# Head 0's row maxima moved forward into the projection stage of a fused attention and expert kernel

## The reference, cut to what matters

```python
mod = (silu(c) @ wmod).reshape(2, 6, 1, -1)
sa, ca, ga, sb, cb, gb = (mod[:, i] for i in range(6))
h = layernorm(x) * (1 + ca) + sa                 # x: (2, 2048, 256)
Q, K, V = lora_linear(h, ...)                    # W x + b + 2 * B(A x), 16 heads of 16
attn = softmax(Q @ K.T / 4); x = x + ga * lora_linear(attn @ V, ...)
h = layernorm(x) * (1 + cb) + sb
x = x + gb * (shared_ffn(h) + routed_ffn(h))     # each row to one of 8 experts
```

## Time and profile before

| | us |
|---|---|
| median of 3 runs (lowest, highest) | 1971.74 (1971.08, 1971.88) |
| the profiled execution, its own time | 1971.86 |
| its span, first to last instruction | 1969.9 |
| busy: TensorE, VectorE, ScalarE, GpSimd | 1867.0, 1570.3, 1244.8, 344.1 |
| one reduce of a 128x512 tile (mean of 2048) | 0.682 |

### The profile page before, as it was taken

The page is one execution under the profiler, slowest core; times in us unless marked ns, Lnnn a source line. Parts: engine busy times, 40 slices in busy tenths (PEclk is TensorE's granted clock), DMA queues, the critical chain, the costliest instruction groups (busy, mean ns, idle before and its releaser), DMA issues.

```text
span 1969.9 us, 34636 instructions
## 1 busy us (share of the span) xinstructions
PE 1867.0 (95%) x13114; PEld 769.8 (39%) x13115; DVE 1570.3 (80%) x2738; ACT 1244.8 (63%) x1423; POOL 344.1 (17%) x429
## 2 busy tenths in 40 slices
PE   8796999999999999999999999999984899999997
PEld 5441222222222222222222222222224655589996
DVE  6765999999999999999999999999826632245553
ACT  5353777777777777777777777777871221144442
POOL 6562200000000000000000000000015622223332
PEclk9997999999999999999999999999997899999998
DMA  5432111111111111111111111111047432322221
GB/s 183 142 129 59 42 41 42 61 55 42 41 54 59 46 41 43 59 57 42 42 54 58 50 39 39 57 54 42 7 150 226 160 102 96 113 82 73 72 72 48
DMA packets 88657, 141.53 MB, mean 72 GB/s; under 512 B 11928, under 2 KB 59032, under 8 KB 88520
## 3 DMA queue, kind: packets, MB, share of 16 engines
q1 hardware_dynamic: 72424, 101.61, 16.0%
q0 software_dynamic: 11072, 32.80, 5.0%
q10 hardware_dynamic: 5024, 5.24, 0.8%
HBM read 90.84 MB, written 48.51 MB: 71 GB/s over the span
## 4 chain that ended last, share of the span: by engine, by line
PE 83%; DVE 10%; DMA 2%; ACT 2%; issue 2%; POOL 1%; SPq 1%; POOLq 0%; DVEq 0%; ACTq 0%
PE ps L943 24%; PE ps L932 20%; PE ps L909 15%; PE ps L1621 7%; DVE mx L999 6%; PE ps L1172 5%; PE ps L1644 3%; PE ps L1506 3%; PE ps L619 2%; DMA l_in<-inverse_sums 2%; PE ps L628 1%; ACT prob L1024 1%; DVE x_t L451 1%; DVE x L1258 1%; PE ps L977 0%
## 5 line engine op out<-in xcount | busy, mean ns | idle before, releaser
L999 DVE TENSOR_REDUCE mx<-ps 128x1 f32<-128x512 f32 x2048 | 1273.7, 682 | 59.5 <-PE ps L909 56.2
L1024 ACT ACTIVATE prob<-ps 128x1024 f32<-128x1024 f32 x1024 | 992.4, 1021 | 275.1 <-PE ps L932 272.6
L943 PE MATMUL ps<-prob,vs 128*32 128x512 f32 x4096 | 546.4, 605 | 0.7 <-ACT prob L1024 0.7
L909 PE MATMUL ps<-k_high,q_high 64*128 64x512 bf16 x2048 | 399.8, 387 | 10.4 <-DVE mx L999 10.4
L932 PE MATMUL ps<-q_high,k_high 64*128 64x512 bf16 x2048 | 390.2, 378 | 15.4 <-issue 12.5
L932 PE MATMUL ps<-q_low,k_low 34*128 34x512 bf16 x2048 | 390.5, 378 | 0.0
L909 PEld LDWEIGHTS ps<-k_high,q_high 64*128 64x128 bf16 x2048 | 99.0, 92 | 646.8 <-DVE mx L999 623.0
L1078 POOL CAST mb<-turned_sb 16x128 bf16<-16x128 f32 x32 | 8.9, 279 | 934.2 <-ACT turned_sb L1037 892.9
L932 PEld LDWEIGHTS ps<-q_low,k_low 34*128 34x128 bf16 x2048 | 100.0, 94 | 117.0 <-issue 0.7
L932 PEld LDWEIGHTS ps<-q_high,k_high 64*128 64x128 bf16 x2048 | 101.5, 96 | 101.6 <-ACT prob L1024 30.0
L943 PEld LDWEIGHTS ps<-prob,vs 128*32 128x32 f32 x4096 | 80.7, 108 | 118.7 <-issue 113.4
(11 more groups left out here) (152 smaller groups left out, 1431.0 us busy)
## 6 DMA issues: line engine op xcount, KB each, us to landing
k_high<-qk_parts SPq DMA_DIRECT2D x126, 128.0 KB
qk_parts<-parts SPq DMA_DIRECT2D x32, 384.0 KB, 3.1
k_low<-qk_parts SPq DMA_DIRECT2D x128, 64.0 KB
head_out<-head_out_sb SPq DMA_DIRECT2D x32, 256.0 KB, 10.8
q_high<-qk_parts SPq DMA_DIRECT2D x126, 64.0 KB
sorted_in<-zero_row POOLq DMA_DIRECT2D x13, 390.0 KB, 7.3
xs<-sorted_in SPq DMA_DIRECT2D x39, 130.0 KB
q_low<-qk_parts SPq DMA_DIRECT2D x64, 64.0 KB
```

Source lines behind the costliest of these rows:

```text
L909: pe.matmul(ps[:, ring.bank((n, m, u)), :], q_high[p][mine, t * P:(t + 1) * P], k_high[p][mine, c * CH:(c + 1) * CH], start=True, stop=Tru ...
L943: mm = pe.matmul(ps[32 * j:32 * j + 32, 7, :], vs[buf(h)][:, kt, :], prob[:, kt % 2, j * CH:(j + 1) * CH], start=(kt == 0), stop=(kt == KT ...
L999: dve.tensor_reduce(mx[n % 2][:, at, c:c + 1], ps[:, ring.bank(what), :], AX.X, ALU.max).then_inc(s_ring, 1)
L1024: act.activation(prob[:, kt % 2, :].rearrange("p (u c n) -> p u c n", u=2, c=2)[:, :, half, :], ps[:, 2 * half:2 * half + 2, :], ACT.Exp). ...
```

## The change

It moves work, and adds or removes no arithmetic.

- **Pairs.** Head 0's 32 pairs: 3 in chunk 2, 4 in chunk 3, 8 in each of chunks 4 to 6, 1 in chunk 7. Two of each eight stand between the two halves of a `qk` unit. Chunk 7 also has 9 pairs of head 1 (`BESIDE`); the other 3 of the 12 follow it.
- **Modulation rows.** The four blocks stand in chunk 7, in banks 0 and 1; ScalarE copies them between its `take`s.
- **Head 0's maxima.** Folded, turned, copied and split within chunk 7; SyncE sends them between the stores of units 1 and 2 of chunk 7. Head 2's operands and the three weights follow the last store.
- **Fills.** The six memsets of `k_low` go to VectorE, ahead of the first `moments`; those of `vs` stay on GpSimd but stand at its start.
- **Head 0's high parts.** The four DMAs of GpSimd go to ScalarE, after it has taken the ninth and tenth unit; it waits there for the first eight stores.
- **Normalizations.** Chunks 4 to 7 are normalized right after the `v` evictions of chunks 0 and 1.
- **Adapters.** Two of the first loads get a semaphore of their own, so the first adapter matmuls wait for two loads, not five.
- ScalarE waits for the last `last_part` before head 0's exponentials (`act.wait_ge(s_qf_free, UQ + UQ * NCH)`). `stage`, `split_maxima`, `negate`, `take_turned` and `maxima` are the old functions, moved out; `take_modulation` is the old copy of a modulation block.

```diff
@@ -463,6 +466,8 @@
...
+            for dst, src in adapters:
+                sp.dma_start(dst[:], src).then_inc(s_adapters, 16)
             for dst, src in first_loads[:-1]:
...
@@ -506,8 +511,9 @@
...
         def setup_tensor(pe):
+            pe.wait_ge(s_adapters, 16 * len(adapters))
+            adapt(pe, 0)
             pe.wait_ge(s_const, 16 * (len(first_loads) - 1))
-            adapt(pe, 0)
             pe.wait_ge(s_wmod, 16)
...
@@ -532,6 +538,10 @@
...
             dve.sem_inc(s_eps, 1)
+            for p in range(NB):
+                for u in range(2):
+                    step(dve.memset(k_low[p][u * HROWS + LROWS:u * HROWS + LROWS + 2, :], 1.0))
+            dve.sem_inc(s_rows, 1)
             moments(dve, step, 0)
...
@@ -603,22 +613,32 @@
...
                 sp.dma_start(dst[:], src).then_inc(s_late, 16)
-            for g in range(CPB, NCH):
+            for g in range(CPB, NCH - 1):
                 store(g, *range(UQ))
-            stack(sp, (0, 2))
-            for dst, name in ((wgT, "wgT"), (wuT, "wuT"), (wdT, "wdT")):
-                sp.dma_start(dst[:], io[name]).then_inc(s_shared, 16)
+            store(NCH - 1, 0, 1)
+            maxima(sp, (0, 0))
+            store(NCH - 1, 2, 3)
...
-            def qk(g, o):
+            def qk(g, o, pair=None):
                 n = unit(g, o)
...
                 for k in range(HALF):
+                    if k and pair is not None:
+                        max_pair(pe, (0, 0), pair)
                     mm = pe.matmul(ps[:, 2 + n % 2, :], wqkv[:, o // 2, k, (o % 2) * P:(o % 2 + 1) * P],
...
                 mm.then_inc(s_unit, 1)
+            def modulation(c):
+                wait(pe, s_mod, c - 1)
+                for k in range(HALF):
+                    mm = pe.matmul(ps[:, c % 2, :], cB[:, k, c // 2, :],
+                                   wmod[:, k, (c % 2 + 1) * 512:(c % 2 + 2) * 512], start=(k == 0), stop=(k == 1))
+                mm.then_inc(s_mrow, 1)
...
@@ -637,31 +657,62 @@
...
             pe.wait_ge(s_weff, 2)
-            for g in range(CPB - 1):
+            for g in range(CPB - 2):
                 qk(g, 1)
...
                 v(g, 1)
+            g = CPB - 2
+            qk(g, 1)
+            v(g, 0)
+            max_pair(pe, (0, 0), 0)
+            qk(g, 3)
+            max_pair(pe, (0, 0), 1)
+            v(g, 1)
+            max_pair(pe, (0, 0), 2)
+            g = CPB - 1
             turn_chunk(pe, CPB)
             for i in range(2):
-                qk(CPB - 1, 1 + 2 * i)
-                for m in range(2):
-                    max_pair(pe, (0, 0), 4 * i + m)
-                v(CPB - 1, i)
-                for m in range(2, 4):
-                    max_pair(pe, (0, 0), 4 * i + m)
-            for g in range(CPB, NCH):
-                if g + 1 < NCH:
-                    turn_chunk(pe, g + 1)
+                qk(g, 1 + 2 * i)
+                max_pair(pe, (0, 0), 3 + 2 * i)
+                v(g, i)
+                max_pair(pe, (0, 0), 4 + 2 * i)
+            for g in range(CPB, NCH - 1):
+                turn_chunk(pe, g + 1)
                 pe.wait_ge(s_hT, g + 1)
                 for i in range(2):
-                    first = 8 + 6 * (g - CPB) + 3 * i
-                    qk(g, 2 * i)
-                    max_pair(pe, (0, 0), first)
+                    m = 7 + 8 * (g - CPB) + 4 * i
+                    qk(g, 2 * i, m)
+                    max_pair(pe, (0, 0), m + 1)
                     qk(g, 2 * i + 1)
-                    max_pair(pe, (0, 0), first + 1)
+                    max_pair(pe, (0, 0), m + 2)
                     v(g, i)
-                    max_pair(pe, (0, 0), first + 2)
+                    max_pair(pe, (0, 0), m + 3)
+            g = NCH - 1
+            pe.wait_ge(s_hT, NCH)
+            pe.wait_ge(s_crow, 1)
+            pe.wait_ge(s_wrow, 16)
+            qk(g, 0)
+            max_pair(pe, (0, 0), PAIRS - 1)
+            modulation(0)
+            max_pair(pe, (0, 1), 0)
+            qk(g, 1)
+            max_pair(pe, (0, 1), 1)
+            v(g, 0)
+            max_pair(pe, (0, 1), 2)
+            turn_maxima(pe, (0, 0))
+            modulation(1)
+            max_pair(pe, (0, 1), 3)
+            qk(g, 2)
+            max_pair(pe, (0, 1), 4)
+            modulation(2)
+            max_pair(pe, (0, 1), 5)
+            qk(g, 3)
+            max_pair(pe, (0, 1), 6)
+            v(g, 1)
+            max_pair(pe, (0, 1), 7)
+            modulation(3)
+            max_pair(pe, (0, 1), 8)
...
@@ -715,13 +772,26 @@
...
                 middle(unit(g, 1))
-            for g in range(CPB, NCH):
-                if g + 1 < NCH:
-                    modulate(g + 1)
+                if g == 0:
+                    parts_stored(act, EARLY)
+                    stack_high(act, (0, 0), 1, s_stack_first)
+            for g in range(CPB, NCH - 1):
+                modulate(g + 1)
                 for o in range(UQ):
...
                     middle(unit(g, o) - 1)
+            for o in range(UQ):
+                take(NCH - 1, o)
+                middle(unit(NCH - 1, o) - 1)
+                if o == 1:
+                    take_turned(act, 0)
+                take_modulation(o)
             middle(UQ * NCH - 1)
+        V_AFTER = {1: (2, 1), 3: (3, 0), 5: (3, 1)}
+        for g in range(CPB, NCH - 1):
+            V_AFTER[7 + 8 * (g - CPB) + 2] = (g, 0)
+            V_AFTER[7 + 8 * (g - CPB) + 6] = (g, 1)
...
@@ -735,34 +805,31 @@
...
             dve.wait_ge(s_bv, 16)
-            for g in range(CPB - 1):
+            for g in range(2):
                 v(g, 0)
-                if g == 0:
-                    normalize(dve, step, CPB)
+                normalize(dve, step, CPB + 2 * g)
                 v(g, 1)
-                normalize(dve, step, CPB + g + 1)
-            for i in range(2):
-                reduce_pair(dve, (0, 0), 4 * i)
-                reduce_pair(dve, (0, 0), 4 * i + 1)
-                v(CPB - 1, i)
-                reduce_pair(dve, (0, 0), 4 * i + 2)
-                reduce_pair(dve, (0, 0), 4 * i + 3)
-            for g in range(CPB, NCH):
-                for i in range(2):
-                    first = 8 + 6 * (g - CPB) + 3 * i
-                    reduce_pair(dve, (0, 0), first)
-                    reduce_pair(dve, (0, 0), first + 1)
-                    v(g, i)
-                    reduce_pair(dve, (0, 0), first + 2)
+                normalize(dve, step, CPB + 2 * g + 1)
+            v(2, 0)
+            for m in range(PAIRS - 1):
+                reduce_pair(dve, (0, 0), m)
+                if m in V_AFTER:
+                    v(*V_AFTER[m])
+            reduce_pair(dve, (0, 0), PAIRS - 1)
+            for m in range(BESIDE):
+                reduce_pair(dve, (0, 1), m)
+                if m == 0:
+                    negate(dve, 0)
+                if m == 1 or m == 6:
+                    v(NCH - 1, m // 6)
...
             pool.sem_inc(s_qf_free, UQ)
-            pool.wait_ge(s_norm, 2)
             for p in range(NB):
-                for u in range(2):
-                    step(pool.memset(k_low[p][u * HROWS + LROWS:u * HROWS + LROWS + 2, :], 1.0))
-            pool.sem_inc(s_rows, 1)
+                pool.sem_inc(s_mrows[p], 64)
+                step(pool.memset(vs[p][:], 0.0))
+                step(pool.memset(vs[p][:, :, DH:DH + 1], 1.0))
...
@@ -779,15 +846,15 @@
...
             last_part(EARLY - 1)
-            for p in range(NB):
-                step(pool.memset(vs[p][:], 0.0))
-                step(pool.memset(vs[p][:, :, DH:DH + 1], 1.0))
-            remainder(EARLY)
-            parts_stored(pool, EARLY)
-            stack_high(pool, (0, 0), 1, s_stack_first)
-            for n in range(EARLY + 1, UQ * NCH):
+            for n in range(EARLY, UQ * NCH):
                 remainder(n)
-                last_part(n - 1)
+                if n > EARLY:
+                    last_part(n - 1)
+                if n == UQ * CPB + 3:
+                    pool.wait_ge(s_vbank_free, 1 + 2 * CPB)
+                    stage(pool, (0, 0))
+                if n == UQ * NCH - 3:
+                    split_maxima(pool, step, 0)
             last_part(UQ * NCH - 1)
...
@@ -870,13 +938,15 @@
...
                 if last >= 1:
-                    maxima(plus(h, 1))
+                    maxima(sp, plus(h, 1))
                 if last == 1:
...
-            maxima((0, 0))
-            maxima((0, 1))
+            stack(sp, (0, 2))
+            for dst, name in ((wgT, "wgT"), (wuT, "wuT"), (wdT, "wdT")):
+                sp.dma_start(dst[:], io[name]).then_inc(s_shared, 16)
+            maxima(sp, (0, 1))
             for n in range(1, NH):
...
@@ -969,19 +1039,8 @@
...
             pe.wait_ge(s_rows, 1)
-            pe.wait_ge(s_crow, 1)
-            pe.wait_ge(s_wrow, 16)
-            max_pair(pe, (0, 1), 0)
-            for n in range(2 * B):
-                for k in range(HALF):
-                    mm = pe.matmul(ps[:, n, :], cB[:, k, n // 2, :],
```

(65 more changed lines are left out.)

32 lines of the change are left out of this document (19 added, 13 removed).

## The result

| | us |
|---|---|
| median of 5 runs after (lowest, highest) | 1960.07 (1958.25, 1963.12) |
| median of 5 runs before, same chip | 1971.74 (1969.25, 1972.51) |
| ratio, 95% interval | 0.9945 (0.9931 to 0.996) |
| the profiled execution after, its span | 1958.25, 1956.3 |

The change brings 11.7 us where 23.7 were forecast; the time lies 2 us above the range of 1939 to 1958. What the forecast said of chunks 4 to 7 came out to a tenth of a us. The loss lies in the first 86 us: one wait for a DMA, and fills that take longer than their recorded durations.

A forecast was written before the change was run, and what follows sets the result against it. TensorE was taken to bound the projection's chunks, with an idle gap before head 0's scores. Terms -12.5, -4.8, -2.2, +4.4 and -8.6 sum to -23.7, from 1971.86 to 1948.2 us; range 1944 to 1953, with rivals 1939 to 1958.

The forecast's parts named there:

- step 4: Start of the kernel: six fills on VectorE delay `moments(0)` to 12.2 us; second half of projection 4.4 us later.
- step 5: Chunks 0 to 3, second half: VectorE stalls, waits for banks and slow clock mostly go, -8.6 us.
- step 3: After the gap: clock stays at 1.00 from the first scores into the attention, -2.2 us.
- Step 1: Gap ahead of head 0's scores: maxima sent within chunk 7 close it wholly, -12.5 us.
- Step 2: Chunk 4 to the scores: pairs between groups no longer wait for VectorE to free banks, -4.8 us.
- Rival (d): Projection: pairs between groups stall on VectorE for banks, 33 us, slower than before at 1981; chance 0.03.
- Rival (a): Start of the kernel: fills on VectorE are fast or hidden, 6.5 us less, 1942; chance 0.15.
- rival (b): Chunk 1 or 2: normalizations meet GpSimd's runs, the long wait returns, step 5 shrinks to about -1, 1956; chance 0.15.
- rival (c): Gap moved: maxima late, or head 0's operands late for chunk 2's first pair; 5 to 10 us back; chance 0.07.
- 3.8 us of slack: Ahead of head 0's scores: they start 3.8 us after the maxima are there; held against rival (c).

The follow-up runs named there:

- e4: The kernel before, with only SyncE sending head 0's maxima ahead of head 2's operands and the three weights: 1957.47 us, ratio 0.9938.
- e10: The changed kernel with e8's fills and e6's sender, plus 12 pairs of head 1 in chunk 7 instead of 9: 1944.03 us, ratio 0.9863.
- e1: The changed kernel with the six `k_low` fills back on GpSimd, behind the second normalization: 1955.04 us, ratio 0.9923.
- e8: The changed kernel with VectorE's fills as 1024 f32 words, three ahead of `moments(0)` and three behind the fourth chunk's normalization: 1951.57 us, ratio 0.9898.
- e5: The changed kernel with ScalarE's four DMAs of head 0's high parts issued by GpSimd, SyncE's four kept: 1956.17 us, ratio 0.9917.
- e6: The changed kernel with all eight DMAs of head 0's high parts issued by GpSimd: 1953.13 us, ratio 0.9904.

## Why the prediction was wrong, and what of it held

| from, to | forecast change | measured (profiles) |
|---|---|---|
| step 4: start to first `v` of the second half | +4.4 | +8.4 |
| step 5: that to chunk 4 | -8.6 | +0.7 |
| steps 1 and 2: chunk 4 to first scores | -17.3 | -17.4 |
| step 3: clock after the first scores | -2.2 | -0.8 |
| sum | -23.7 | -9.1 |

The medians differ by 11.7, 2.6 more than these 9.1. The rest lies behind the change, inside the 1791 to 1796 of the table above, where kernels that share all this code differ by as much. The two profiled executions differ by 13.6 and show where: from the third turn to the same weighting at the attention's end it is 1244.16 us in before (187.07 to 1431.23) and 1244.15 in after (177.98 to 1422.13), so the attention kept its pace as forecast. The other 4.5 us lie in the stages behind it, which the change doesn't touch; there the granted clock of three stretches of 50 us was 0.88, 0.77 and 0.80 in before (from 1437.07) and 0.91, 0.78 and 0.86 in after (from 1427.98). What makes it differ there no run shows.

**Step 1, right.** Maxima were counted to leave 17.1 us after chunk 7's start and left at 159.26 - 141.99 = 17.3; scores were counted at 26.2 and came at 26.0. The cover held, and the last waits are VectorE's 0.8 for a bank. That SyncE's order alone made the gap, as the prediction read from 149.63 and 162.71, e4 shows: its chunk 4 to first scores is 12.6 us shorter than before's (76.9 against 89.5), where 12.5 were forecast.

**Step 2, right.** 15.37 us a chunk against 15.3 counted, VectorE 11.40 against 11.4, and no pair in chunks 4 to 6 waits for a bank. From chunk 4 to the scores after is 4.8 us shorter than e4 (72.1 against 76.9), as forecast. Rival (d), slower than before, didn't appear.

**Step 3, wrong, by 1.4 us.** The forecast made the gain hang on the clock staying at 1.00, and took three pauses between pairs for too few to lower it. They are all that stands ahead of its fall in after, so its reason may well hold, with three being enough. But e10 shows that it isn't the only one: without these pauses the clock still falls, behind the wait for the first exponentials. That this wait does it there is argued, since no run took it away.

**Step 4, a term mis-sized.** The duration was forecast to the hundredth (1.77, recorded 1.76), but six of them were put 0.03 apart where they stand 0.49 apart, and the first begins at 2.00 instead of 1.41: 13.2 us instead of 10.8, `moments(0)` at 15.16 instead of 12.2. The rows 6 that I took give one fill of each size, and no row of two long fills in sequence; the duration of one isn't what the next one waits. The other 1.0 us is that less of the delay was absorbed than counted. Rival (a), fast fills, is out: putting the fills elsewhere gives 7.6 us at the scores in e1, and elsewhere and half as long 10.5 in e8.

The Trainium skill, in VectorE: DVE Perf Modes, section "Zero memsets can be issued as uint32 (trn2)", gives one cycle per element for a fill. At the 0.96 GHz of the page's section "Specifications" that is an estimate of 2.13 us for 2048, nearer to the spacing of 2.25 than to the recorded 1.76, and its advice to fill in words of four bytes is what e8 does with a value that isn't zero.

**Step 5, the step that failed.** It forecast -8.6 and measured +0.7. Its own content was about right: `v` waits 2.03 us once instead of 6.89, normalizations take 4.76, 1.38, 1.38 and 3.93 where 9.58 stood, and rival (b) didn't come. But the step let the first pair start when TensorE reaches it, and never asked when its operands land. That was rival (c) in its second half, to which I gave 0.07 together with another case, against "3.8 us of slack", which belonged to the maxima and not to these loads. What stood in its place is a wait of 10.29 us for head 0's operands, and about 1.6 us of half clock behind it (80.04: 3.52 instead of 1.9); without these 11.9 the step would have brought 11.2, more than forecast.

Two edits made the wait. One moves four of the eight DMAs from GpSimd's queue to ScalarE's, and was costed by ScalarE's issue time alone; e5 takes it back and still waits 4.40, e6 sends all eight from GpSimd, waits 2.02 and gives 9.4 us back at the scores. The other lets TensorE reach its first pair sooner. Counted from the first `v` of the second half, that pair's turn came after 31.6 us in before (at 74.47, in chunk 3, behind the stall for `v`) and 18.0 us in after (69.21, in chunk 2), while the last operand landed after 22.3 us (65.2) and 28.1 us (79.4). In before the landing lay within the stall that the change removes, and 9.3 us ahead of its use.

## To carry to other kernels

A DMA that is moved to another engine's queue has a new landing time, not only a new issue time: look for its landing in the trace and for the DMA share of a stretch where nothing else moves, and where that share is a small multiple of 1/16, try another queue, as e6 did here with GpSimd's (a wider outermost dimension was not tried). When a stall goes, ask of every transfer that landed during it when it is next wanted. Measure the simplest part alone first: here one reordering of a queue had the gain of the whole change, and the rest added its 15 us only together with two repairs.

## What the runs showed of the hardware that was not expected

- Eight loads of 64 to 128 KB with an outermost dimension of 2 took 19.6 us from SyncE's and ScalarE's queues with 2.1 of 16 DMA engines busy from 72.50 to 75.00, and 12.4 us from GpSimd's, with 0.88 of all 16 busy from 70.00 to 72.50.
- A fill of 2 x 2048 bf16 on VectorE is recorded with 1.76 us and takes 2.25 start to start, with or without a semaphore between; 1024 f32 words take 0.91 and 1.16.
- TensorE's clock fell from 1.00 to 0.50 of 2.4 GHz at 168.5 in after, behind 20.87 us without a pause (142.90 to 163.77) and three pauses of 0.80 to 0.87 us, and before its wait for the first exponentials. In e10, without these three, it held through a wait of 2.04 us and fell 1.5 us after it (155.4).
